# Scaling a skip term on ScalarE and opening PSUM sums with transposes, in a pipelined two-layer transformer kernel

## What is computed

```python
x, z = jnp.split(hidden_states @ in_proj_w.T, 2, axis=-1)
x = silu(conv(x) + conv_b)                      # 512 channels
dt, k, q = jnp.split(x @ x_proj_w.T, [64, 80], axis=-1)
def step(state, inp):                           # state: 512 channels x 16
    x_t, dt_t, k_t, q_t = inp
    dtv = sigmoid(dt_t @ dt_head_w.T + dt_head_b)
    dtv = dtv / (1.0 + dtv * sum(k_t * k_t))
    state = state * (1.0 - dtv * k_t * k_t) + (x_t * dtv) * k_t
    return state, einsum('bdn,bn->bd', state, q_t)
y = scan(step, ...) + D * x                     # D * x is the skip term
out = (y * silu(z)) @ out_proj_w.T
```

## Time and profile before

| | |
|---|---|
| median of 3 runs | 1822.53 us (1820.58 to 1823.0) |
| the profiled execution | 1821.96 us, of which the span is 1820.2 us |
| busy share of the span | PE 91%, DVE 81%, ACT 72%, POOL 75% |
| mean granted TensorE clock | 0.979 of full speed |
| turns 1 to 14 | about 79 us each |

### The profile page before, as it was taken

How to read it: one execution, slowest core, us unless ns; L and a number is a source line. 1 busy time by engine, 2 the same in 40 slices (tenths; PEclk the granted TensorE clock), 3 DMA queues, 4 the chain that set the end, 5 groups by cost and what they waited for, 6 DMA issues and landing times.

```text
span 1820.2 us, 33709 instructions
## 1 busy us (share of the span) xinstructions
PE 1657.9 (91%) x12156; PEld 1424.5 (78%) x12156; DVE 1469.9 (81%) x3084; ACT 1314.7 (72%) x2689; POOL 1369.6 (75%) x644
## 2 busy tenths in 40 slices
PE   6678999999999999999999999997777999999998
PEld 5557788887878888787878878786665888899997
DVE  3548889898988988898898889889897678766663
ACT  3568878888887888878788888876643855666664
POOL 0009899999989999999999999999998343444443
PEclk9899999999999999999999999999997999999999
DMA  5011111212111221221122122112112444455552
GB/s 198 1 56 44 71 66 71 73 68 83 68 68 65 76 83 54 82 76 60 65 76 83 53 83 76 59 61 97 65 70 93 116 128 99 122 139 140 137 136 29
DMA packets 69462, 149.78 MB, mean 82 GB/s; under 512 B 5936, under 2 KB 43312, under 8 KB 68912
## 3 DMA queue, kind: packets, MB, share of 16 engines
q1 hardware_dynamic: 57008, 130.84, 20.7%
q0 software_dynamic: 12288, 16.79, 5.2%
HBM read 121.91 MB, written 17.30 MB: 76 GB/s over the span
## 4 chain that ended last, share of the span: by engine, by line
PE 63%; DVE 14%; ACT 12%; issue 6%; POOL 4%; DMA 0%; DVEq 0%; ACTq 0%; POOLq 0%
PE po L1834 10%; PE ph L1834 9%; DVE room L1179 8%; PE pD L1130 8%; PE pY L1147 7%; PE pA L731 6%; POOL room L1188 3%; PE pB L926 3%; PE pB L936 3%; PE pB L1226 3%; ACT room L1160 2%; PE pA L722 2%; PE pB L957 2%; PE pB L942 2%; PE pA L652 1%
## 5 line engine op out<-in xcount | busy, mean ns | idle before, releaser
L1198 POOL TENSOR_TENSOR room<-room 128x1024 f32<-128x1024 f32 x256 | 608.2, 2376 | 159.4 <-DVE room L1113 139.0
L1179 DVE TENSOR_TENSOR_SCAN room<-pD,last,room 128x256 f32<-128x256 f32 x1024 | 688.7, 731 | 38.3 <-PE pD L1130 26.0
L1188 POOL TENSOR_TENSOR room<-room 128x1024 f32<-128x1024 f32 x256 | 607.8, 2375 | 46.4 <-PE pY L1147 46.2
L1160 ACT ACTIVATE room<-room,kkT 128x512 f32<-128x512 f32 x512 | 359.8, 715 | 57.4 <-PE pD L1130 55.9
L1130 PE MATMUL pD<-fixed,room 128*128 128x128 f32 x2048 | 318.1, 279 | 70.1 <-DVE room L1179 60.5
L1147 PE MATMUL pY<-fixed,room 128*128 128x128 f32 x2048 | 315.6, 277 | 15.1 <-POOL room L1188 15.0
L1130 PEld LDWEIGHTS pD<-fixed,room 128*128 128x128 f32 x2048 | 239.1, 143 | 103.2 <-issue 53.4
L1147 PEld LDWEIGHTS pY<-fixed,room 128*128 128x128 f32 x2048 | 246.2, 144 | 66.8 <-POOL room L1188 30.8
L343 POOL DMA_INDIRECT xg<-xn_rows,W x64 | 67.5, 1055 | 196.5 <-DVE W L337 180.9
L1793 ACT ACTIVATE h<-ph 128x512 f32<-128x512 f32 x128 | 76.6, 598 | 137.9 <-PE ph L1834 101.4
L1834 PE MATMUL po<-w_up,h_up 128*128 128x256 f32 x512 | 149.5, 292 | 3.2 <-DVE h_rest L1701 2.6
(11 more groups left out here) (313 smaller groups left out, 3400.0 us busy)
## 6 DMA issues: line engine op xcount, KB each, us to landing
room<-kq_rows SPq DMA_DIRECT2D x128, 512.0 KB, 3.6
w_in<-w_d SPq DMA_DIRECT2D x32, 1024.0 KB
room<-ndS SPq DMA_DIRECT2D x16, 512.0 KB, 3.2
xt<-x_in SPq DMA_DIRECT2D x16, 256.0 KB, 2.9
y_out<-xo SPq DMA_DIRECT2D x16, 256.0 KB, 2.1
xn_rows<-xnC SPq DMA_DIRECT2D x16, 256.0 KB, 2.2
W<-weights SPq DMA_DIRECT2D x1, 1808.0 KB, 8.8
W<-weights SPq DMA_DIRECT2D x1, 1697.5 KB, 16.4
```

The source lines that it names most:

```text
L1160: act.activation(decT[:, m % 2, t, :], turn2(ndT, it, NT * DI, t * DI, DI), ACT.Copy, bias=1.0, scale=turn2(kkT, it, NT * DS, t * DS + m, ...
L1179: dve.tensor_tensor_scan(run, pD[h][:, k2 * TB:(k2 + 1) * TB], run, last[:, bass.ds(later(it) * (DS * DT) + m * DT + k, 1)], ALU.mult, ALU ...
L1188: pool.tensor_tensor(sq[:, m % 2], st[:, m % 4], kqb[:, m % SLOTS, 1, :].unsqueeze(1).broadcast_to([P, DT, TB]), ALU.mult).then_inc(sem("r ...
L1198: pool.tensor_tensor(st[:, m % 4], turn2(u, it, DT * TB).rearrange("p (k t) -> p k t", k=DT), kqb[:, m % SLOTS, 0, :].unsqueeze(1).broadca ...
```

## The change

The skip term is scaled before the transposition instead of by it. ACT multiplies each group of `xs` by its 128 values of D (one scale for each partition) and writes `xd`, which lies in the last quarter of `w_in`. `AT["xd"]` = 56: the four groups come at steps 56, 58, 60 and 62 of the turn that makes `xs`. The opening of `pY` then transposes `xd` with the identity. The diagonal matrices are no longer made, and SP waits for the last opening before the second half of the first expert's weights overwrites `xd`.

```diff
-    scan=13, rd=23, inp=14)
+    scan=13, rd=23, xd=56, inp=14)
...
-        dskip = sb("dskip", [P, DT, P])
...
+        xd = w_in[:, 3 * H * TB:4 * H * TB].rearrange("p (k t) -> p k t", k=DT)
...
+            k = (n - AT["xd"]) // 2
+            if 0 <= k < DT and (n - AT["xd"]) % 2 == 0:
+                act.wait_ge(sem("opened"), it * 2)
+                act.wait_ge(sem("xs"), it * 2 + k // 2 + 1)
+                act.activation(xd[:, k, :], xs[:, k, :], ACT.Copy, scale=w("dskip")[:, k:k + 1]).then_inc(sem("xd"), 1)
...
                 if n == AT[f"open{t}"]:
-                    pe.wait_ge(sem("xs"), it * 2 + 2)
+                    pe.wait_ge(sem("xd"), it * DT + DT)
                     pe.wait_ge(sem("yz"), it * 2 - 1 + t)
                     for k in range(DT):
-                        i = pe.matmul(pY[:, t, k * P:(k + 1) * P], xs[:, k, t * P:(t + 1) * P], dskip[:, k, :],
-                                      start=(k == 0), stop=False, skip_group_check=True)
+                        i = pe.matmul(pY[:, t, k * P:(k + 1) * P], xd[:, k, t * P:(t + 1) * P], ident_s[:, :],
+                                      start=(k == 0), stop=False, is_transpose=True, skip_group_check=True)
...
-                for k in range(DT):
-                    dve.tensor_scalar(dskip[:, k, :], fx("ident"), w("dskip")[:, k:k + 1], None, ALU.mult)
...
                 for half in range(2):
+                    if half == 1:
+                        sp.wait_ge(sem("opened"), NB * 2 + 2)
                     load_half(sp, sem, 0, half, w_in, w_ds)
```

More of the change, by code:

```diff
@@ L81 @@
     k_turn=1, kk=3, dt_mm=2, sig=2, den_ln=1, den=1, ndt=1, nd_in=16, ut_mm=2, u=2,
-    inp=DS, dec_t=2 * DS, dec_mm=2 * DS, scanned=DT * DS, saved=DS, read_out=DS, summed=2 * DS, opened=2,
+    inp=DS, dec_t=2 * DS, dec_mm=2 * DS, scanned=DT * DS, saved=DS, read_out=DS, summed=2 * DS, opened=2, xd=DT,
     yz=2, y_turn=2, yT=2, glast=1, out_mm=1, score_mm=1, scores=1)
```

## The result

The changed kernel takes 1840.95 us in the median of 4 runs (1838.32 to 1843.13), the kernel before 1821.55 us (4 runs): a ratio of 1.0106 (95% interval 1.0087 to 1.0124), so it is slower by 1.1%. I had said 1838.5 us, in a range from 1829 to 1843. The profiled execution took 1839.38 us, its span 1837.6 us, against 1821.96 and 1820.2 before.

What follows compares the result with a forecast made beforehand. The bound was taken as a 79.04 us loop of waits across engines, with the copies on ACT's piece. Copies 16.2 us minus 0 for openings, on 1821.96, gave 1838.2, stated as 1838.5 us; range 1829 to 1843.

Steps and rivals of the forecast that it cites:

- The chain and the place of the copies: Loop of waits through PE, ACT, DVE and POOL, 79.04 us a turn; copies cost only where ACT has no wait.
- ACT's piece of the chain: End of a turn: table load of `sg`, decay piece, L803; copies two to four were said to delay ACT by 1.20 us.
- the one in the wait: First copy, in ACT's 0.74 us wait for PE ahead of the second `sig`; claimed to cost nothing.
- The price of a copy: Each 128x256 scaled copy on ACT: 0.50 us busy, 0.40 us added to the queue, bounds 0.31 and 0.50.
- the rival of dearer copies: Copies cost 0.50 us each, two standing next to a table load: 20.7 us in all, 1843 us; chance 0.09.
- The delay of `og`: DVE's `og` starts 1.06 us later in turns 1 to 13, 1.20 in turns 0 and 14: 16.2 us together.
- a slack of 0.14: In the steady turn `og` could have started at 998.74 after L809, but started at 998.88.
- The openings give nothing back: Transposes save PE 0.45 us at each of 32 openings; claimed worth 0 to the chain, upper bound 5.9 us.
- the wait for POOL: PE's 0.30 us wait ahead of the first `sum`; the first opening's 0.45 us was to lengthen it to 0.75.
- The rival in which it counts in full: The second opening, step 24, saves its full 0.45 us a turn: +10.3 us, 1833 us; chance 0.14.
- PE's total work: Rival: PE's queue decides and ACT's work is hidden, so 14.2 us are saved, 1808 us; chance 0.05.
- The sum: 13.8 us for turns 1 to 13 plus 2.4 for turns 0 and 14, openings 0: 16.2 us slower.

Runs made afterwards that it cites:

- DVE relieved: Changed kernel with copies at steps 45, 45, 46, 50 and DVE's `x_scan` at step 36 instead of 28: 1817.30 us, ratio 0.9987 to the kernel before.

## Why the prediction was right

*The chain and the place of the copies.* Right. The three copies that stand on ACT's piece of the chain delay it by their time, and the one in the wait costs none. The fourth copy made twice costs 0.39 a turn, the first nothing, and all four in waits nothing.

*The price of a copy,* 0.50 us busy, 0.40 in the queue. Measured 498 ns and 0.39 to 0.41. Ahead of the table load it was 0.40 too, so the rival of dearer copies is out.

*The delay of `og`,* the larger of two copies and of three less a slack of 0.14: 1.06 predicted, 1.11 measured. Two copies gave 0.80 with the fourth moved away. The slack was as I had read it: counted from the addition to x one turn earlier (922.60 before, 936.06 now), L809 ends at 76.04 before and 77.27 now, 1.23 later, and `og` starts at 76.28 and 77.37, 1.09 later. What I had too small is the three copies together, 1.23 instead of 1.20, and a few hundredths behind `og`.

*The openings give nothing back.* Right in the turns, for both reasons. The first runs into the wait for POOL. The second runs into DVE, which I had at step 33 alone and which comes last at step 31 as well; with DVE relieved the 0.47 came out. The rival in which it counts in full is out for the kernel as changed. Over the whole time the openings did worse than nothing, which I had not foreseen: by the medians the transposes cost 3.4 us alone, and some 2 to 3 in the other pairs that differ in them alone.

*PE's total work.* Out: 128 products turned to transposes left a turn at 79.02 us. Here no engine's total decides, and ACT's 64 instructions were worth 0 or 1.1 us a turn by their place. The Trainium skill ("Perfetto Trace Analysis", Identifying the Most-Contended Engine) says to optimize the engine of highest occupancy first, TensorE judged by its weight loads. By that, work should leave PE (78%) or DVE (81%) rather than ACT (72%); the turns don't bear it out.

*The sum.* From the two profiles: the twelve distances from step 4 of turn 2 to that of turn 14 give 13.6 us, where I had 12 x 1.06 = 12.7 (a longer turn more is in it). Turn 14 gives 1.26 (1.20). Up to step 4 of turn 2 it is 214.49 - 210.97 = 3.5 us, where I had 1.20 + 1.06 = 2.3 and not the 1.2 that transposes cost in turn 1. The end is 1.0 shorter, where I had nothing. Together 17.4 against 16.2. The medians differ by 19.4, 3 more than my 16.2. The copies alone make 17.2 of them. What I had put at nothing is the effect of the transposes outside the steady turns, 2 to 3 us, which is shown by the medians and whose cause stays open; the granted clock at the start and at the end, which I had not in the sum at all, moves single profiles by as much. That the range held the result is partly luck: its upper end was there for dearer copies. Two small slips changed nothing. The 0.57 added to 1838.2 makes 1838.7 or more and not 1838.5. And the 15 table loads of `sg` are those of turns 0 to 14; a sixteenth at 55.1 us comes ahead of any copy.

## What to carry to other kernels

Where the work of several engines forms a loop, ask of each instruction moved from one engine to another on which piece of the loop it lands, and put it into a wait of the receiving engine that is long enough to hold it; the same four copies cost 1.1 us a turn or nothing. In this kernel a saving on the engine that the chain names was worth only as much as the slack that the engine beside it had at the next point where they met: look for the load or the scan that ends within a tenth of a microsecond of it. When that companion is found, relieve it first, and measure the relief alone and with the saving.

## What was not expected of the hardware

The granted clock was at full level from 170 to 1240 us in every kernel, and fell at times between 30 and 170 us and behind 1240 us. There, two profiles with the same instructions differed by 3.9 us from the last addition to x to the end (578.9 and 582.8 us); after the same wait of 2.60 us the clock fell in one and not in the other. Moving a sum on DVE by eight steps, which costs 0.1 us in a turn, made the median 4.0 us longer. On a span of 1820 us, a difference of 0.2% between two versions of this kernel says little of the edit itself; the distance of a turn in the profile, which mostly repeats to 0.03 us, says it better.
